# FFN 2 fused with router logits 1, linear attention fused with the reload and router logits 2, and a threshold search with two bits a round

## The chip, the cores and the metric

One core of a Trainium2 chip. The metric is device time in microseconds of one execution, the median of the runs. Engines: PE (TensorE), DVE (VectorE), ACT (ScalarE), POOL (GpSimd), SP (SyncE, which issues the plain DMAs).

## The reference

4096 tokens (4 batches of 1024) of 256 channels pass through six residual blocks in float32:

```
x = x + 0.5 * ffn(layernorm(x))
x = x + attention_over_sets(layernorm(x))
x = x + 0.5 * ffn(layernorm(x))          # FFN 2
x = x + 0.5 * moe(layernorm(x))          # routed experts, first time
x = x + linear_attention(layernorm(x))   # per batch: relu(q), relu(k), kv = k^T v
x = x + 0.5 * moe(layernorm(x))          # the same experts, second time
# inside moe, for the rows xf of layernorm(x), T = 4096, E = 32, cap = 160:
ri = concat(xf, mean, std, min, max, l2, share of |xf| < 1e-6)
h = gelu(ri @ r1_w.T + r1_b)
probs = softmax(h @ r2_w.T);  topp, topi = top_k(probs, 2)
score = where(routed, probs, -inf)
idx = argsort(-score, axis=0)[:cap].T    # each expert keeps its best 160 tokens
```

Each expert then runs a gated FFN on its 160 tokens, adds an adapter shared by two experts, and the weighted rows are added back to the tokens.

## The kernel before

The program is a row of stages (`Stage`), each with its own buffers and semaphores; a stage ends with a barrier of all engines. Inside a stage every engine runs its own list in order and waits on semaphores. x stays in SBUF as `x_res`, 32 tiles of 128 tokens; a group is 4 tiles, a batch 8. PSUM is 8 banks.

- `ffn` (L198 on): DVE normalizes a group (L194), PE transposes (L203), ACT copies (L294), PE multiplies (L270), POOL adds the bias (L226), DVE adds the product to x (L240) and takes the statistics (bn_stats, L163). Two groups are in flight.
- `moe` calls `route`, `experts` and, the first time, `reload`. `route` begins with the router front: variance over all 32 tiles on DVE (L171 to L183), one power on POOL for rstd (L188), two for the moments (L1341), then per group DVE norm, minimum, maximum (L1476, L1477) and the count under 1e-6 (L1480) from ACT's absolute value (L1367), PE's transposes, `hidden` (L1406, L1407), ACT's gelu (L1371), PE's logits (L1414) and DVE's copy of them (L1488). SP sends the expert weights first, then the rows of the normalized x, then x itself.
- The route proper begins at L1509: softmax, two picks a token, and the scores of 32 experts laid over 128 partitions (4 chunks an expert, 1024 columns). The search then finds each expert's 160th score bit by bit: 30 rounds, each a count by DVE, a sum over the four chunks by PE, and two small DVE operations:

```
nc.vector.tensor_scalar(above[:], score[:], thr[:].bitcast(F32), None, ALU.is_ge, ALU.add,
                        accum_out=count[:, 0:1]).then_inc(counted, 1)
v.wait_ge(totaled, k + 1)
```

- Behind the search come places, lists and indices for the gathers; `experts` runs 32 experts in quads, with weights loaded four experts ahead.
- `reload` (L1858) brings x back from `x_sum` in DRAM and takes its statistics. `linear_attention` takes one variance and one power over all tiles, then loops over the batches: norm, transposes (L2003), keys and values (L1974) with the running sum of k^T v (L1983), queries, the product with the output weights, the outputs (L1974), and DVE's update of x (L1945, L1946, L1948) with bn_stats (L1951). POOL adds the bias to the batch in one operation (L1918). PE runs ahead of DVE by the banks that it finds free.

Of the kernel before, what the change touches and what calls it, by code (L numbers as in the profile page):

```python
# [9 lines left out]

# [13 lines left out]
P = 128  # L24
# [4 lines left out]
GT = 4  # L29
# [1138 lines left out]
class RouterSetup:  # L1168
# [17 lines left out]
    def constants(self, nc, pool):  # L1186
# [22 lines left out]
        chain.link(nc.gpsimd.memset(s.half[:], 0.5))  # L1209

# [8 lines left out]
def alloc_moe(nc, s):  # L1219
# [12 lines left out]
    s.half = sb("half", [P, TILES], F32)  # L1232
    s.xn_rows = nc.dram_tensor("xn_rows", (TOKENS, ROW), F32, kind="Internal").ap()
# [3 lines left out]
def moe(nc, s, name, up_dram, down_dram, aup_dram, adown_dram, out=None):  # L1237


    st = Stage(nc, name)  # L1240
    w_up = [st.sb(f"w_up{k}", [P, CC, 2 * INTER]) for k in range(EQ)]
    w_down = [st.sb(f"w_down{k}", [P, INTER // P, C]) for k in range(EQ)]
    a_up = [st.sb(f"a_up{k}", [P, CC, 2 * A_INTER]) for k in range(EQ // 2)]
    a_down = [st.sb(f"a_down{k}", [P, C]) for k in range(EQ // 2)]
    of_pick = st.sb("of_pick", [P, QUADS_E, ST_TILES, 2])
    gather_i = st.sb("gather_i", [P, SLOT_TILES], I32)
    scatter_i = st.sb("scatter_i", [P, QUADS_E * 2 * ST_TILES], I32)
    w_in = [st.sem(f"w_in{k}") for k in range(EQ)]
    a_in = [st.sem(f"a_in{k}") for k in range(EQ // 2)]
    x_kept = st.sem("x_kept")  # L1250
    total = s.x_sum if out is None else out

    def load_expert(sp, e, k):

        sp.dma_start(w_up[k][:], up_dram[bass.ds(e, 1)].rearrange("o p c j -> (o p) c j")).then_inc(w_in[k], 16)
        sp.dma_start(w_down[k][:], down_dram[bass.ds(e, 1)].rearrange("o p c j -> (o p) c j")).then_inc(w_in[k], 16)

    def load_adapter(sp, g, k):
        sp.dma_start(a_up[k][:], aup_dram[bass.ds(g, 1)].rearrange("o p c j -> (o p) c j")).then_inc(a_in[k], 16)
        sp.dma_start(a_down[k][:], adown_dram[bass.ds(g, 1)].rearrange("o p j -> (o p) j")).then_inc(a_in[k], 16)  # L1260

    route(nc, s, name + "r", of_pick, gather_i, scatter_i, total, x_kept, load_expert, load_adapter)
    experts(nc, s, name + "e", w_up, w_down, a_up, a_down, w_in, a_in, of_pick, gather_i, scatter_i, total, x_kept,
            load_expert, load_adapter)
    if out is None:
        reload(nc, s, name + "c")
    st.close()
# [841 lines left out]
```

## Time and profile before

| | us |
|---|---|
| median of 3 timed runs | 2075.1 |
| lowest, highest | 2064.27, 2077.95 |
| the profiled execution | 2061.07 |
| its span | 2059.4 |
| busy in the span: PE | 1526.4 (74%) |
| DVE | 977.2 (47%) |
| ACT | 583.5 (28%) |
| POOL | 550.4 (27%) |

Mean granted TensorE clock 0.861 of full speed. Times of rows are from the start of the span. A row of a timeline gives start, busy time, engine, line, operation and tiles, and in brackets how long the engine had been idle and who ended that. "x8" means that eight like instructions in a row are merged in one line.

### The profile page before, as it was taken

The numbers are of one execution on the slowest core, as the hardware profiler recorded it, in microseconds if no ns is written. First come the engines' busy times: TensorE is split into PE (matmuls) and PEld (weight loads), VectorE is DVE, ScalarE is ACT, GpSimd is POOL, SyncE is SP. The second block draws the span as 40 slices with busy tenths as digits, with TensorE's granted clock in tenths as the row PEclk, the third lists the DMA queues.
The fourth block names the chain that finished last, engine by engine and source line by source line (L and its number), as shares of the span: only waits on it lengthen the run. The fifth ranks groups of instructions, "written<-read, shape, count | busy, mean of one in ns | idle before, by whom it ended". The sixth has DMA issues, their size and how long they took to land. (4 is left out here: it accounts for less than half of the span.)

```text
span 2059.4 us, 26489 instructions
## 1 busy us (share of the span) xinstructions
PE 1526.4 (74%) x9242; PEld 1139.1 (55%) x9242; DVE 977.2 (47%) x2391; ACT 583.5 (28%) x1295; POOL 550.4 (27%) x418
## 2 busy tenths in 40 slices
PE   2699889999996672238998894599763237999894
PEld 2567534545444541228898893356432226898894
DVE  5765677777754677671111110444367682111110
ACT  0122146665662141002323321111132002323321
POOL 2542200000003502002446336110111002346346
PEclk9899889999998886558999997799877557999997
DMA  2024463432100332004778774300133003778874
GB/s 90 16 87 136 103 111 59 77 72 50 45 2 1 121 105 81 0 0 141 221 215 231 228 189 52 104 0 0 63 136 102 5 0 101 241 209 212 254 208 51
DMA packets 114031, 212.12 MB, mean 103 GB/s; under 512 B 20149, under 2 KB 79962, under 8 KB 104730
## 3 DMA queue, kind: packets, MB, share of 16 engines
q1 hardware_dynamic: 87066, 178.93, 27.6%
q0 software_dynamic: 26880, 32.13, 10.4%
q8 instruction: 45, 0.74, 0.2%
q14 instruction: 40, 0.33, 0.1%
HBM read 158.71 MB, written 51.90 MB: 102 GB/s over the span
## 5 line engine op out<-in xcount | busy, mean ns | idle before, releaser
L907 DVE TENSOR_REDUCE attnm_top<-psum 128x1 f32<-128x384 f32 (+3 forms) x384 | 215.8, 596 | 70.6 <-PE psum L996 65.5
L1131 ACT ACTIVATE attnm_prob<-psum 128x512 f32<-128x512 f32 (+1 forms) x384 | 192.4, 530 | 132.5 <-PE psum L1006 127.3
L1843 DVE SCALAR_TENSOR_TENSOR moe1e_h<-moe1e_gate,psum 128x160 f32<-128x160 f32 x160 | 51.3, 321 | 261.6 <-ACT moe1e_gate L1801 261.6
L1718 POOL DMA_INDIRECT x_sum<-moe1e_y,moe_scatter_i x80 | 124.9, 1561 | 178.2 <-ACT moe1e_y L1825 112.4
L1843 DVE SCALAR_TENSOR_TENSOR moe2e_h<-moe2e_gate,psum 128x160 f32<-128x160 f32 x160 | 51.3, 321 | 252.5 <-ACT moe2e_gate L1801 252.5
L1718 POOL DMA_INDIRECT out<-moe2e_y,moe_scatter_i x80 | 125.1, 1564 | 170.0 <-ACT moe2e_y L1825 100.7
L1773 PE MATMUL psum<-moe1e_xgT,moe_w_up 128*128 128x160 f32 x1024 | 155.9, 314 | 10.4 <-issue 8.3
L1773 PEld LDWEIGHTS psum<-moe1e_xgT,moe_w_up 128*128 128x128 f32 x1024 | 151.0, 202 | 12.8 <-issue 12.8
L1773 PE MATMUL psum<-moe2e_xgT,moe_w_up 128*128 128x160 f32 x1024 | 150.4, 306 | 8.3 <-issue 6.1
L1773 PEld LDWEIGHTS psum<-moe2e_xgT,moe_w_up 128*128 128x128 f32 x1024 | 145.6, 196 | 10.1 <-issue 10.1
L994 PE MATMUL psum<-attn_mask_ts,ident_bf 128*128 128x128 bf16 x512 | 106.4, 228 | 15.5 <-DVE attnm_top L907 10.5
L893 POOL TENSOR_TENSOR attnm_tail_v<-attnm_v_tail,attnm_tail_p 128x256 f32<-128x256 f32 x32 | 19.8, 620 | 364.0 <-DVE attnm_on L954 299.3
L994 PEld LDWEIGHTS psum<-attn_mask_ts,ident_bf 128*128 128x128 bf16 x512 | 48.8, 99 | 114.9 <-issue 57.1
L996 PE MATMUL psum<-attnm_k_hat,attnm_q_hat 96*128 96x512 bf16 (+3 forms) x384 | 106.8, 306 | 0.0
L1006 PE MATMUL psum<-attnm_q_hat,attnm_k_hat 99*128 99x512 bf16 (+1 forms) x288 | 98.3, 344 | 0.0
L1019 PE MATMUL psum<-attnm_prob,attn_v_aug 128*32 128x512 f32 (+1 forms) x768 | 88.8, 533 | 0.0
L1801 ACT ACTIVATE moe1e_gate<-psum 128x160 f32<-128x160 f32 x160 | 48.5, 303 | 139.0 <-PE psum L1773 139.0
L1801 ACT ACTIVATE moe2e_gate<-psum 128x160 f32<-128x160 f32 x160 | 48.5, 303 | 131.1 <-PE psum L1773 131.1
L1785 PE MATMUL psum<-moe1e_h,moe_w_down 128*128 128x160 f32 x512 | 80.4, 300 | 2.6 <-ACT moe1e_yT L1808 2.6
L1785 PE MATMUL psum<-moe2e_h,moe_w_down 128*128 128x160 f32 x512 | 80.4, 300 | 2.6 <-ACT moe2e_yT L1808 2.6
L1785 PEld LDWEIGHTS psum<-moe2e_h,moe_w_down 128*128 128x128 f32 x512 | 72.9, 190 | 3.6 <-issue 3.6
L1785 PEld LDWEIGHTS psum<-moe1e_h,moe_w_down 128*128 128x128 f32 x512 | 72.9, 190 | 3.6 <-issue 3.6
(409 smaller groups left out, 2983.7 us busy)
## 6 DMA issues: line engine op xcount, KB each, us to landing
moe_w_up<-in_expert_up SPq DMA_DIRECT2D x64, 1024.0 KB, 5.6
moe_w_down<-in_expert_down SPq DMA_DIRECT2D x64, 512.0 KB, 7.0
attnm_q_hat<-q_parts SPq DMA_DIRECT2D x72, 128.0 KB, 4.8
moe_a_up<-in_adapter_up SPq DMA_DIRECT2D x32, 256.0 KB, 6.8
q_parts<-attnf_q_part SPq DMA_DIRECT2D x12, 512.0 KB, 2.8
attnm_k_hat<-k_parts SPq DMA_DIRECT2D x72, 64.0 KB, 2.3
x_res<-in_x SPq DMA_DIRECT2D x8, 512.0 KB, 8.5
v_tails<-attnf_v_tail SPq DMA_DIRECT2D x4, 1024.0 KB, 4.1
```

What stands on the lines that cost most here:

```text
L893: nc.gpsimd.tensor_tensor(tail_v[:, k % 2].rearrange("p (h d) -> p h d", d=HD), v_tail[:, b % 2, k].rearrange("p (h d) -> p h d", d=HD), t ...
L907: nc.vector.tensor_reduce(top[:, n // QUADS % 2, tiles[0]:tiles[-1] + 1, hh:hh + 1], s.ps[:, u.bank, 0:len(tiles) * width].rearrange("p (t ...
L994: nc.tensor.matmul(out[:, width - P:width], s.identb[:], o.mask_ts[:, tile % 2, :], start=(i == 0), stop=False, skip_group_check=True)
L996: ins = nc.tensor.matmul(out, q_hat[r][0:MROW, h, tile * P:(tile + 1) * P], k_hat[r][0:MROW, h, 0:width], start=False, stop=True, skip_gro ...
L1006: nc.tensor.matmul(s.ps[:, u.bank, at:GROUP], k_hat[r][0:MROW + NPART, h, j * P:(j + 1) * P], q_hat[r][0:MROW + NPART, h, g * GROUP + at:( ...
L1019: ins = nc.tensor.matmul(s.ps[32 * h:32 * h + 32, u.bank, at:GROUP], o.v_aug[:, first:first + 32], prob[:, i % NPROB, at:GROUP], start=(j ...
L1131: nc.scalar.activation(prob[:, i % NPROB, at:GROUP], s.ps[:, u.bank, at:GROUP], ACT.Exp).then_inc(taken[u.bank], 1)
L1718: nc.gpsimd.indirect_dma_start(total, bass.IndirectOffsetOnAxis(ap=scatter_i[:, at:at + 1], axis=0), y[:, q, k, :], None, bounds_check=TOK ...
L1773: ins = nc.tensor.matmul(s.ps[:, u.bank, half * CAP:(half + 1) * CAP], lhsT, xgT[:, q, c, k * CAP:(k + 1) * CAP], start=(c == 0), stop=(c ...
L1785: ins = nc.tensor.matmul(s.ps[:, u.bank, o * CAP:(o + 1) * CAP], lhsT, h[:, n % 2, i, :], start=(i == 0), stop=(i == PAIRS - 1))
L1801: nc.scalar.activation(gate[:, i, :], s.ps[:, u.bank, 0:CAP], ACT.Silu).then_inc(silu, 1)
L1843: nc.vector.scalar_tensor_tensor(out=h[:, n % 2, i, :], in0=gate[:, i, :], scalar=1.0 if i < INTER // P else SCALE_A, in1=s.ps[:, u.bank, ...
```

## The change

Lines move by one at the top and by more behind; the names of the tiles `moe1r_...` become `ffn_r_...` and `lin_r_...` where the router front moves.

1. The router front becomes a class, `RouterFront`, whose methods each issue one step for one group. Variance and powers are now taken per group (4 columns for rstd, 8 for the moments). The count under 1e-6 goes from DVE to ACT: Abs, Relu(1e-6 - |x|), and four Signs with an accumulator; ACT also copies the logits. SP stores x and the normalized rows group by group.
2. `ffn_router` replaces FFN 2 and the first router front. ACT now normalizes for FFN (Identity with scale and bias), and PE's order is a table.
3. `linear_router` replaces `reload`, `linear_attention` and the second front. Statistics, variance and rstd are taken per batch, the weights are loaded behind the first two groups of x, six PSUM banks rotate over all uses, and the front of batch b - 1 is laid between the steps of batch b.
4. The search takes two bits a round: the scores are split into their upper and lower 16 bits as floats, and a round tests three thresholds at once, one on DVE and two on ACT. POOL's products `value` come after its part of the conversion, so beside the search.

```diff
+    def count(self, act, g, ks):
+        act.wait_ge(self.near_made, g + 1)
...
+        for k in ks:
+            ins = self.nc.scalar.activation(self.size[:, g % 2, k, :], self.near[:, g % 2, k, :], ACT.Sign,
+                                            accum_out=self.stat[:, g % 2, k, 4:5])
...
+def ffn_router(nc, s, name, m):
...
+    for i in range(-2, GROUPS + 4):
+        for what, g in (("turn", i + 2), ("multiply", i + 1), ("turn_s", i - 2), ("hidden", i - 2), ("logits", i - 3), ("turn_x", i - 1)):
...
+            for i in range(GROUPS + 2):
+                if i < GROUPS:
+                    update(i)
+                    r.var(chain, i)
+                if i >= 2:
+                    r.finish(v, i - 2)
+                if 1 <= i <= GROUPS:
+                    r.moments(v, chain, i - 1)
+                    for k in range(GT):
+                        r.norm(v, i - 1, k)
+                    r.extremes(v, i - 1)
...
+            for i in range(-3, GROUPS + 4):
+                if 0 <= i + 3 < GROUPS:
+                    norm(i + 3)
+                if 0 <= i + 2 < GROUPS:
+                    copy(i + 2)
+                if 0 <= i - 2 < GROUPS:
+                    r.copy_s(act, i - 2)
+                    r.gelu(act, i - 2)
+                if 0 <= i - 3 < GROUPS:
+                    r.take(act, i - 3)
+                if 0 <= i - 1 < GROUPS:
+                    r.absolute(act, i - 1)
+                    r.under(act, i - 1)
+                    r.count(act, i - 1, range(GT))
+                    r.copy_x(act, i - 1)
...
-    ROUNDS = 30
...
+    HIGH = [4 ** k for k in range(6, -1, -1)]
+    LOW = [4 ** k for k in range(7, -1, -1)]
...
+                for i in (1, 3):
+                    ins = nc.scalar.activation(junk[i // 2], score[:], ACT.Sign, bias=tries[:, i:i + 1], scale=-1.0,
+                                               accum_out=under[:, i // 2 + 1:i // 2 + 2])
+                ins.then_inc(signed, 1)
...
+                pe.wait_ge(counted, k + 1)
+                pe.wait_ge(signed, k + 1)
+                nc.tensor.matmul(s.ps[:, 5, 0:3], s.same_e[:], under[:], start=False, stop=True).then_inc(totaled, 1)
...
+                    v.wait_ge(totaled, done + k + 1)
+                    chain.link(nc.vector.tensor_scalar(passed[:], s.ps[:, 5, 0:3], 0.0, None, ALU.is_le, ALU.add,
+                                                       accum_out=steps[:]))
...
+    def use():
+        return banks.use(next(ring) % 6)
...
+                for k in range(BT):
+                    ins = update(b, k)
+                    if k % GT == GT - 1:
+                        chain.link(ins)
+                        r.var(chain, BG * b + k // GT)
+                    if k == 2 and b >= 1:
+                        r.finish(v, r1)
+                if b + 2 < BATCH:
+                    stats(b + 2)
```

PE in FFN 2 and the router front, a middle stretch. Before, these are two stages, and in FFN 2 the row reads:

```order
L203 MATMUL psum<-ident,ffn_xn 128x128 x16
L270 MATMUL psum<-ffn_w,ffn_xnT 128x256 x8
L203 MATMUL psum<-ident,ffn_xn 128x128 x8
L270 MATMUL psum<-ffn_w,ffn_xnT 128x256 x8
L203 MATMUL psum<-ident,ffn_xn 128x128 x8
```

In the change one turn of the steady state reads so (the first two rows are FFN's for later groups, then the statistics, `hidden`, logits and transposes of earlier ones):

```order
L204 MATMUL psum<-ident,ffn_xn 128x128 x8
L1559 MATMUL psum<-ffn_w,ffn_xnT 128x256 x8
L1432 MATMUL psum<-ident,ffn_r_stat 5x128 x4
L1441 MATMUL psum<-ffn_r_xnT,r 128x512 x2
L1442 MATMUL psum<-ffn_r_statT,r1s 128x512
L1449 MATMUL psum<-r,ffn_r_hT 128x32 x4
L1423 MATMUL psum<-ident,ffn_r_xn 128x128 x8
```

The front's five PE steps now stand between FFN's multiply of one group and the transposes of the next.

PE in linear attention, the end of a batch, before (output of the batch is the last two rows, 8 tiles in all):

```order
L1974 MATMUL psum<-lin_w,lin_kvT 128x256 x4
L2033 REGISTER_ALU
L1974 MATMUL psum<-lin_kvw,lin_qT 128x257 x8
L1972 REGISTER_ALU
L1974 MATMUL psum<-lin_kvw,lin_qT 128x257 x4
```

and in the change, for batch 1 and later:

```order
L1423 MATMUL psum<-ident,lin_r_xn 128x128 x8
L2321 MATMUL psum<-lin_xnT,lin_w 128x512 x4
L2321 MATMUL psum<-lin_w,lin_kvT 128x256 x4
L2321 MATMUL psum<-lin_kvw,lin_qT 128x257 x6
L1432 MATMUL psum<-ident,lin_r_stat 5x128 x4
L1441 MATMUL psum<-lin_r_xnT,r 128x512 x2
L1442 MATMUL psum<-lin_r_statT,r1s 128x512
L2321 MATMUL psum<-lin_kvw,lin_qT 128x257 x6
```

The previous batch's router work stands between the queries and between the outputs (the second group's follows in the same way, then both logits).

DVE in the search, one round before:

```order
L1554 TENSOR_SCALAR moe1r_above,moe1r_count<-moe1r_score,moe1r_thr 128x1024
L1558 TENSOR_SCALAR moe1r_drop<-psum 128x1
L1559 SCALAR_TENSOR_TENSOR moe1r_thr<-moe1r_drop,moe1r_thr 128x1
L1554 TENSOR_SCALAR moe1r_above,moe1r_count<-moe1r_score,moe1r_thr 128x1024
L1558 TENSOR_SCALAR moe1r_drop<-psum 128x1
```

and the start and first round of the change:

```order
L1784 TENSOR_SCALAR moe1r_n_above<-moe1r_score 128x1024
L1785 TENSOR_SCALAR moe1r_n_equal<-moe1r_score 128x1024
L1807 COPY moe1r_level<-moe1r_tries 128x1
L1789 TENSOR_SCALAR moe1r_above,moe1r_under<-moe1r_score,moe1r_tries 128x1024
L1792 TENSOR_SCALAR moe1r_ahead<-tries_no,moe1r_tries 128x4
L1796 TENSOR_SCALAR moe1r_passed,moe1r_steps<-psum 128x3
L1798 SCALAR_TENSOR_TENSOR moe1r_tries<-moe1r_steps,moe1r_ahead 128x4
L1789 TENSOR_SCALAR moe1r_above,moe1r_under<-moe1r_score,moe1r_tries 128x1024
```

A round keeps one count on DVE; the two others are ACT's, between the same two waits.

## Rows read from the trace of the kernel before

**Rows 1.** Table of stretches; columns as its first line names them.
```profile
core 0: us, PE busy (x) PEld busy (x) DVE busy (x) ACT busy (x) POOL busy (x), PEclk, DMA share, GB/s
703.00:785.00 82.00, 48.16 (x208) 27.82 (x208) 47.15 (x152) 28.33 (x34) 16.82 (x4) 0.79 0.53 189
...
814.80:885.60 70.80, 17.58 (x60) 15.05 (x60) 48.17 (x121) 0.00 (x0) 1.55 (x1) 0.50 0.04 4
...
1303.00:1484.00 181.00, 161.01 (x560) 100.49 (x560) 73.21 (x219) 28.59 (x72) 23.59 (x6) 0.95 0.02 7
```

**Rows 2.** Timeline of FFN 2 (start us, us, engine, line, operation), one group.
```profile
675.17 2.37 POOL L226 TENSOR_TENSOR x_res<-x_res,ffn_bias 128x1024 f32 x1 [5.73 <-DVE ffn_xn L194]
...
675.25 1.22 DVE L240 TENSOR_TENSOR x_res<-x_res,psum 128x1024 f32 x1 [0.27 <-PE psum L270]
...
675.97 3.62 PE L270 MATMUL psum<-ffn_w,ffn_xnT 128*128 128x256 f32 x16
...
676.17 1.02 ACT L294 COPY ffn_xnT<-psum 128x1024 f32<-128x1024 f32 x1 [3.42 <-PE psum L203]
```

**Rows 3.** Timeline, router front 1, one group.
```profile
761.08 1.88 PE L1406 MATMUL psum<-moe1r_xnT,r 128*128 128x512 f32 x4
...
761.28 0.57 ACT L1361 COPY moe1r_statT<-psum 5x512 f32<-5x512 f32 x1 [0.23 <-PE psum L1397]
...
764.05 0.69 ACT L1371 ACTIVATE moe1r_hT<-psum,r1b 128x512 f32<-128x512 f32 x1 [2.20 <-PE psum L1407]
...
764.64 1.05 ACT L1367 ACTIVATE moe1r_work<-moe1r_xn 128x1024 f32<-128x1024 f32 x1
...
764.79 1.08 PE L1414 MATMUL psum<-r,moe1r_hT 128*128 128x32 f32 x8 [0.78 <-ACT moe1r_hT L1371]
```

**Rows 4.** Timeline, powers before both stages; the route's first reduction.
```profile
653.34 5.46 POOL L188 TENSOR_TENSOR rstd<-var_eps,minus_half 128x32 f32<-128x32 f32 x1 [9.68 <-DVE var_eps L183]
...
712.29 10.92 POOL L1341 TENSOR_TENSOR moe1r_moment<-moe1r_moment,half 128x32 f32<-128x32 f32 x2 [1.05 <-DVE moe1r_moment L1465]
...
784.50 1.22 DVE L1509 TENSOR_REDUCE moe1r_col<-moe1r_prob 128x32 f32<-128x1024 f32 x1
```

**Rows 5.** Timeline, second round of the first search.
```profile
817.27 1.28 DVE L1554 TENSOR_SCALAR_CACHE_REDUCE moe1r_above<-moe1r_score,moe1r_thr 128x1024 f32<-128x1024 f32 x1
...
818.62 0.59 PE L1433 MATMUL psum<-moe1r_count,same_e 128*128 128x1 f32 x2 [1.77 <-DVE moe1r_above L1554]
...
819.24 0.16 DVE L1558 TENSOR_SCALAR moe1r_drop<-psum 128x1 int32<-128x1 f32 x1 [0.68 <-PE psum L1433]
...
819.62 1.28 DVE L1554 TENSOR_SCALAR_CACHE_REDUCE moe1r_above<-moe1r_score,moe1r_thr 128x1024 f32<-128x1024 f32 x1
```

**Rows 6.** Timeline, from the reload to the second route.
```profile
1285.34 7.96 SPq L1858 DMA_DIRECT2D x_res<-x_sum  x8
...
1290.33 11.69 DVE L163 BATCH_NORM_STATS2 x_stats<-x_res 128x6 f32<-128x256 f32 x32 [39.29 <-DMA x_res<-x_sum]
...
1311.59 3.68 PE L2003 MATMUL psum<-ident,lin_xn 128*128 128x128 f32 x16 [52.21 <-DVE lin_xn L194]
...
1336.20 2.66 DVE L194 TENSOR_SCALAR lin_xn<-x_res,mean,rstd 128x256 f32 x8
...
1361.09 1.13 PE L1983 MATMUL psum<-lin_v_row,lin_k_row 128*128 128x257 f32 x4 [0.46 <-DVE lin_k_row L1929]
...
1377.69 2.66 DVE L194 TENSOR_SCALAR lin_xn<-x_res,mean,rstd 128x256 f32 x8
...
1482.15 0.43 DVE L1951 BATCH_NORM_STATS2 x_stats<-x_res 128x6 f32<-128x256 f32 x1
...
1566.01 1.22 DVE L1509 TENSOR_REDUCE moe2r_col<-moe2r_prob 128x32 f32<-128x1024 f32 x1
```

**Rows 7.** FFN 2's norm line (ns min/median/max); norms of router front 1.
```profile
L194 DVE TENSOR_SCALAR ffn_xn<-x_res,mean,rstd x12: 400/404/2464, 658.8 to 666.5; 128x256 f32<-128x256 f32 x8, 128x256 f32 x4
...
712.12 2.67 DVE L194 TENSOR_SCALAR moe1r_xn<-x_res,mean,rstd 128x256 f32<-128x256 f32 x8
```

More of the change, by code:

```diff
@@ L11 @@
+import itertools
 from contextlib import ExitStack
@@ L1565, in _ @@
+            search(LOW, len(HIGH))
+            chain.link(nc.vector.tensor_copy(level[:], tries[:, 1:2]))
+            nc.vector.tensor_scalar(above[:], score[:], level[:], None, ALU.is_gt, ALU.add, accum_out=count[:, 0:1])
+            nc.vector.tensor_scalar(equal[:], score[:], level[:], None, ALU.is_equal, ALU.add,
                                     accum_out=count[:, 1:2]).then_inc(tied, 1)
@@ new lines, in linear_router @@
+    u_T, u_kv, u_acc, u_q, u_turn, u_kvw, u_out, ring = {}, {}, {}, {}, {}, {}, {}, itertools.count()
+    def use():
+        return banks.use(next(ring) % 6)
+    for what, b, k in ORDER:
+        if what == "turn":
+            for c in range(CC):
+                u_T[b, k, c] = use()
+        elif what == "kv":
+            u_kv[b, k] = use()
+        elif what == "sum":
+            if k == 0:
+                for d in range(CC):
+                    u_acc[b, d] = banks.use(6 + d)
+        elif what == "q":
+            for f in range(CC):
+                u_q[b, k, f] = use()
+        elif what == "turn_kv":
+            u_turn[b] = use()
+        elif what == "kvw":
+            u_kvw[b] = use()
+        elif what == "out":
+            u_out[b, k] = use()
+        else:
+            r.plan(what, b, use)
@@ L1966, in _, with project @@
+            for g in range(BG * (BATCH - 1), GROUPS):
+                r.moments(v, chain, g)
+                for k in range(GT):
+                    r.norm(v, g, k)
+            for g in range(BG * (BATCH - 1), GROUPS):
+                r.extremes(v, g)
+                r.finish(v, g)
         @block.tensor
         def _(pe):
-            pe.wait_ge(w_in, 48)
-            pe.wait_ge(ones_made, 1)
-            def project(u, b, out, pairs):
-                pe.wait_ge(taken[u.bank], u.before(b))
+            def project(u, out, pairs):
+                pe.wait_ge(taken[u.bank], u.before(0))
@@ L2056, in linear_attention @@
+            r0, r1 = GROUPS - 2, GROUPS - 1
+            for g in (r0, r1):
+                r.absolute(act, g)
+                r.under(act, g)
+                r.count(act, g, range(GT))
+                r.copy_x(act, g)
+            for g in (r0, r1):
+                r.copy_s(act, g)
+                r.gelu(act, g)
+            for g in (r0, r1):
+                r.take(act, g)
     st.close()
```

899 lines of the change are left out of this document (600 added, 299 removed).

## The prediction

> **What bounds the kernel now.** The page's chain of waits reaches back only through the last expert stage, which the change leaves as it is, so I read by stretches first. The table of stretches [rows 1] shows three that the change touches: the front of the first router (PE busy 48 of 82 us, DVE 47 of 82: neither is full), the search (DVE busy 48 of 71, ScalarE 0, the granted clock at 0.50, which is the 1.2 GHz level, because PE has almost nothing to do), and linear attention (PE busy 161 of 181 at clock 0.95, close to 2.4 GHz: PE sets the pace). Then the timeline of each. FFN 2 is a ring of GpSimd's bias, PE's multiply, ScalarE's copy and DVE's update [rows 2]. The router front has no full engine; every group passes through DVE, PE and ScalarE in turn [rows 3], and before it begins everybody waits for long powers on GpSimd, one like FFN 2's of 5.46 us and then two in 10.92 us [rows 4]. A search round is a strict chain: count 1.28, a 128x1 matmul 0.59, two tiny DVE operations, and again 2.35 us later (819.62 - 817.27) [rows 5]. Thirty of them are the 70.8 us of rows 1, and the second router repeats them. In linear attention a batch takes 41.5 us (1377.69 - 1336.20), and before PE's first transpose at 1311.59 lie the reload from 1285.34 and 32 statistics in 11.69 us [rows 6].
>
> **Part 1: FFN 2 with router front 1.** Now it ends at 784.50, where the route proper starts [rows 4]. I count the fused stage by its fullest engine, group by group.
> ScalarE gets FFN's normalization (four 128x256 activations, the columns of Abs's 1.05 in four pieces, about 1.5), the copy 1.01, the statistics copy about 0.6, then it stands behind PE's `hidden` (761.08 to gelu's start at 764.05, 2.95) before gelu 0.69, takes the logits 0.3 (behind PE's 1.08), Abs 1.05, Relu 1.0, four accumulating Signs and two halves of the copy 1.1 [rows 2, 3]. No row shows an accumulating ScalarE operation. Below it is a plain one, a quarter of Abs's 1.05 or 0.3 with its start; above, three times that; I take 0.45, 1.8 for four. Sum: 12.4 us a group; 10.9 without the normalization, 9.9 without the first copy (the last groups).
> PE: transposes 1.0, multiply 3.6, transposes again 1.0, statistics 0.5 with 0.7 of waiting for their copy, hidden 2.95, logits 1.0 = 10.7. DVE: update 1.2, four bn_stats 1.4, variance and moments 13 tiny ones of 0.16 to 0.2, 2.4 in all, norm 1.4, minimum and maximum 2.4 (two reductions of 1024 columns at 1.22 [rows 4]), rest 0.4 = 9.2. GpSimd: 2.4 of bias and, at 5.46/32 = 0.17 us a column, 2.1 of powers = 4.5. So ScalarE sets the pace.
> Fill: rstd is ready at about 659 (653.34 and 5.46 [rows 4]), the first hidden ends near 693 (update 0 at 670, norm 0 at 681, counts 685, finish 688, then 4 us on PE). From there 2 x 12.4 + 10.9 + 4 x 9.9 = 75 to the last hidden at 768, 2.5 for the last gelu, logits and copy, 1.1 for the change of stage: 772 against 784.5. **-13 us**, between -26 (DVE's 9.2 as the pace) and +3 (dear Signs).
>
> **Part 2: the reload, linear attention and router front 2.** Now from 1285.34 to 1566.01 [rows 6].
> Start: PE waits for 8 tiles of statistics instead of 32 (24 x 0.365 = 8.8 saved) and for a power over 8 columns instead of 32 (about 4 saved); the change of stage between goes too (1.2), and the weights, now queued behind two groups of x, come about as late as the first transposed tile (0 to 5 lost). -12.6.
> Batch 0: DVE gets two variances (2 x 1.5) and the statistics of batch 2 (8 x 0.365 and 1.4) behind its updates. There is no slack there: PE already waits 0.46 for DVE's next key at 1361.09. +7.3.
> Batches 1 to 3: PE gets per batch two each of transposes 0.95, statistics with their copy 1.1, hidden 2.7 and logits 0.95 = 11.4. It was the pace, so all of it is path. +13 for batch 1 (statistics of batch 3 behind it), +11.4 for batch 2, +8 for batch 3, whose last updates, DVE-bound before, now have only two tiles left to do once PE is through. What hides beside PE: DVE's norm, extremes and finish (some 11 us a batch) and ScalarE's Abs, Relu, Signs (4 us), spread over 55 us. If that cover goes, see the second rival.
> End: from the last update (1482.6) to 1566.01 there are 83.4 us now, the whole front 2. After, only the last two groups: variance, power, moments and norm 4.6 for the first, then ScalarE's 5 for each, the two hidden with gelu 8, logits and copies 2.5, some 26, and 1.2 for the stage. -56.
> Sum: -12.6 + 7.3 + 13 + 11.4 + 8 - 56 = -29. I add 3 for queueing between in-order engines (0 to 20). **-26 us.**
> SP's stores are moved too: 1 MB a group, behind var and norm, on a queue that stands idle then; the expert weights are issued only at the start of the route, a good 100 us before their use. Both cost nothing, and the search is their cover.
>
> **Part 3: the search, twice.** The order shows 7 + 8 = 15 rounds with one DVE count and two ScalarE counts each. No row shows a 128x1024 Sign with accumulation. Below stands Abs at 1.05 [rows 3], two of them overlapped 2.0; above, 1.7 each. I take 2.25 for the pair, near the row. DVE's own 1.28 count hides behind it. The rest of the round stays: from the count's end to the next count 1.06 (matmul 0.59 and the tiny ones), 0.1 for one more accumulator read, 0.06 to start ScalarE. 3.47 x 15 = 52 against 70.7. Added: two integer operations on 1024 columns (0.6 to 1.3 each), one 1.05 conversion and 0.4 small, 3.0; in the middle two DVE passes and a restart, 2.7; the level copy 0.2. 57.9: **-12.8 us** each, between -19 and +8 (4.7 a round). GpSimd's bf16 products now run beside the first rounds instead of beside DVE's last steps ahead of them: I count that as nothing (-2 to +4). Two searches, -25.6.
>
> **Sum.** -13 - 26 - 25.6 = -65. The profiled execution took 2061.1 (its span is 2059.4), the three timed runs 2064.3 to 2078.0 with the median 2075.1, 14 above it. So 1996 for an execution like the profiled one, **2010** for the median.
>
> **The shared port.** One norm of 128x256 in FFN 2 took 2464 ns where its median is 404, just where GpSimd's 2.35 us bias add ran; eight norms under the long power took their usual 2.67 [rows 7]. So a bias add stops DVE's norms and a power does not. The Trainium skill (SBUF — State Buffer, Who interferes with whom) says that a DVE operation in a two-port mode and a GpSimd operation exclude each other for a whole instruction, which speaks against giving GpSimd and DVE more to do side by side. The bias add agrees with it, the power does not. In the fused FFN the bias add falls, by the order, mostly on minimum and maximum; in linear attention on updates that read PSUM. By the trace I add nothing; by the rule it would be the last rival.
>
> **Rivals.**
> 1. ScalarE's accumulator is dear, 0.5 us more for each. FFN: 2 us a group, +16; search: 1.0 a round, 15 x 2, +30; the end of linear attention +4. That leaves 15: 2060. For: nothing shows its price. Against: DVE's own accumulator read is tiny, its 1.28 count being hardly longer than the plain reduction of 1024 columns, 1.22 [rows 4, 5].
> 2. The in-order queues of linear attention hold each other up: PE stands behind turn_s and its copy, ScalarE behind hidden, DVE behind the counts, and each batch is 6 us longer. 47 left: 2028. For: PE already runs 89% busy. Against: six rotating banks.
> 3. Slower: GpSimd blocks DVE with everything it does in the fused stages. FFN 8 x 4.5 = 36; linear attention 4 bias adds of twice 2.37 and 22 of powers, 41; in each search four products and a conversion of 1024 columns, at the bias row's 2.4 each, 12, twice 24: 101 in all, +36: 2111. It turns the sign once more than 65 of the 101 lie on the path. For: the 2464 ns norm. Against: norms under the power.
>
> **How the numbers follow.** Forecast 0.68, rival 1 0.08, rival 2 0.21, rival 3 0.03. A measurement tells about 1% (21 us) from no change. Faster by over 1%: forecast, rival 2 and a fifth of rival 1, 0.91; within 1% 0.06; slower 0.03. The range: with every part at its best, 26, 29 and 2 x 19, they save 93 (1982); upward the range goes past rival 2 to 2042.
>
> **What would show it.** Route 1's first reduce 12 to 14 us earlier after the end of attention (131 us after FFN 2's rstd begins at 653.34 become some 119); search rounds of 3.4 to 3.6 us with ScalarE the last releaser of PE; 255 us from the reload to route 2, batches of 53 to 55. Wrong if a round takes over 4.2, if ScalarE is not the fullest engine of the fused FFN, or if a batch takes 60.

## The result, and the profile after

The changed kernel takes 1999.7 us (median of four runs, 1990.8 to 2004.3), against 2075.9 before in the same runs: the ratio is 0.968, with a 95% interval from 0.963 to 0.972 (the two medians alone would give its lower edge). A second measurement (e5_again below) gave 0.968 again (0.963 to 0.974). The forecast was 2010 of 2075.1, a ratio of 0.969. The profiled execution took 2000.8 (span 1999.1), where 1996 was forecast for an execution like the profiled one of before. ScalarE's busy time rose from 583.5 to 719.5 us:

```profile
PE 1537.6 (77%) x9242; PEld 1145.6 (57%) x9242; DVE 917.0 (46%) x2376; ACT 719.5 (36%) x1625; POOL 564.7 (28%) x454
```

The sum came out; its parts did not all. Between marks that both traces have (times in us):

| Stretch | before | after | difference | forecast |
|---|---|---|---|---|
| start to FFN 2's rstd power | 653.3 | 647.3 | -6.1 | 0 |
| stage 1: from there to route 1's first reduction | 131.2 | 134.7 | +3.6 | -13 |
| route 1, to the count after the search | 101.0 | 86.4 | -14.6 | -12.8 |
| from there to the reload (experts) | 399.8 | 396.2 | -3.6 | 0 |
| reload to route 2 | 280.7 | 247.5 | -33.1 | -26 |
| route 2, to the count after the search | 101.0 | 86.4 | -14.6 | -12.8 |
| from there to the end | 392.4 | 400.5 | +8.1 | 0 |

The three stretches that the change does not touch moved by -6.1, -3.6 and +8.1 and nearly cancel. The first and the last go with the granted clock (from 100 to 300 us it is 0.92 instead of 0.90, in the last 200 us 0.88 instead of 0.93). So a stretch is worth a few us more or less from one execution to the next, and parts are read from their own marks.

**Stage 1.** The table of stretches of the changed kernel, columns as in [rows 1], cut where the last FFN multiply ends (738), and at the end of linear attention:

```profile
core 0: us, PE busy (x) PEld busy (x) DVE busy (x) ACT busy (x) POOL busy (x), PEclk, DMA share, GB/s
647.30:702.00 54.70, 38.14 (x165) 27.61 (x165) 30.81 (x104) 32.35 (x62) 32.08 (x16) 0.81 0.20 68
702.00:738.00 36.00, 32.96 (x158) 24.10 (x158) 22.20 (x68) 23.76 (x54) 9.69 (x6) 0.92 0.26 88
738.00:782.00 44.00, 31.25 (x80) 16.13 (x78) 10.74 (x38) 18.72 (x47) 4.58 (x4) 0.51 0.11 36
...
1485.30:1512.20 26.90, 14.99 (x52) 7.82 (x52) 10.04 (x35) 12.47 (x31) 4.34 (x3) 0.71 0.18 59
```

Two things stand against the prediction. ScalarE is nowhere the fullest engine. And from 738 the granted clock is 0.51, the 1.2 GHz level, in a stretch where nobody is full. The timeline shows group 5 there (start us, us, engine, line, operation, idle time before it and its releaser):

```profile
736.29 0.69 ACT L1408 ACTIVATE ffn_r_hT<-psum,r1b 128x512 f32<-128x512 f32 x1 [3.30 <-PE psum L1442]
...
741.47 0.17 DVE L1365 TENSOR_SCALAR ffn_r_stat<-ffn_r_stat 128x4 f32<-128x4 f32 x1 [1.70 <-ACT ffn_r_size L1383]
...
741.70 1.02 PE L1432 MATMUL psum<-ident,ffn_r_stat 128*5 128x128 f32 x4 [3.53 <-DVE ffn_r_stat L1365]
...
742.75 0.57 ACT L1401 COPY ffn_r_statT<-psum 5x512 f32<-5x512 f32 x1 [0.36 <-PE psum L1432]
743.58 3.75 PE L1441 MATMUL psum<-ffn_r_xnT,r 128*128 128x512 f32 x4 [0.86 <-ACT ffn_r_statT L1401]
747.26 2.07 PE L1442 MATMUL psum<-ffn_r_statT,r1s 5*128 5x512 f32 x2
749.37 0.69 ACT L1408 ACTIVATE ffn_r_hT<-psum,r1b 128x512 f32<-128x512 f32 x1 [6.04 <-PE psum L1442]
```

Read it as a ring, that is, a loop in which each engine waits for what the next one makes from its own last result: ScalarE counts, VectorE finishes, TensorE transposes the statistics, ScalarE copies them, TensorE multiplies (hidden: here 5.8 us, in rows 3 still 3.0), and only the gelu lets ScalarE go on to the next group's Abs, Relu and counts. While ScalarE counts, TensorE waits 3.53; while TensorE multiplies, ScalarE waits 6.04.

**Search.** One steady round of the changed kernel's first search; compare [rows 5]:

```profile
840.15 1.15 ACT L1694 ACTIVATE moe1r_work<-moe1r_score,moe1r_tries 128x1024 f32<-128x1024 f32 x1 [3.39 <-DVE moe1r_tries L1812]
840.15 1.28 DVE L1789 TENSOR_SCALAR_CACHE_REDUCE moe1r_above<-moe1r_score,moe1r_tries 128x1024 f32<-128x1024 f32 x1
...
841.30 1.13 ACT L1694 ACTIVATE moe1r_work<-moe1r_score,moe1r_tries 128x1024 f32<-128x1024 f32 x1
...
842.67 0.56 PE L1711 MATMUL psum<-moe1r_under,same_e 128*128 128x3 f32 x2 [1.91 <-ACT moe1r_work L1694]
843.26 0.16 DVE L1796 TENSOR_SCALAR_CACHE_REDUCE moe1r_passed<-psum 128x3 f32<-128x3 f32 x1 [1.68 <-PE psum L1711]
...
843.66 1.28 DVE L1789 TENSOR_SCALAR_CACHE_REDUCE moe1r_above<-moe1r_score,moe1r_tries 128x1024 f32<-128x1024 f32 x1
```

A round is 843.66 - 840.15 = 3.51 us for two bits, where one bit took 2.35, and what releases TensorE is ScalarE's second count.

**Linear attention.** From the reload to route 2, the rows that answer to [rows 6]:

```profile
1264.68 0.93 SPq L2188 DMA_DIRECT2D x_res<-x_sum  x2
...
1276.14 3.65 PE L2330 MATMUL psum<-ident,lin_xn 128*128 128x128 f32 x16 [38.81 <-DVE lin_xn L195]
...
1318.43 1.81 PE L2330 MATMUL psum<-ident,lin_xn 128*128 128x128 f32 x12
...
1328.88 1.89 PE L2349 MATMUL psum<-lin_v_row,lin_k_row 128*128 128x257 f32 x4 [3.13 <-DVE lin_k_row L2246]
...
1377.68 1.94 PE L2330 MATMUL psum<-ident,lin_xn 128*128 128x128 f32 x16
...
1432.28 1.94 PE L2330 MATMUL psum<-ident,lin_xn 128*128 128x128 f32 x16
...
1485.31 0.43 DVE L2272 BATCH_NORM_STATS2 x_stats<-x_res 128x6 f32<-128x256 f32 x1
...
1512.21 1.22 DVE L1740 TENSOR_REDUCE moe2r_col<-moe_prob 128x32 f32<-128x1024 f32 x1 [14.41 <-PEq L57]
```

From transpose to transpose the batches take 42.3, 59.3 and 54.6 us (41.5 for a batch before), the last one 53.0 to its last update, and from there route 2 is 26.9 us away (83.9 before).

### The profile page after: what moved, and what is told of

Same layout as the page of the kernel before. It is cut to its first block and busy times, and to the rows that moved or that the text cites. A ratio compares the mean times of both kernels' runs of the same rounds, so it can differ in the third digit from the quotient of the medians.

```text
span 1999.1 us, 26485 instructions
## 1 busy us (share of the span) xinstructions
PE 1537.6 (77%) x9242; PEld 1145.6 (57%) x9242; DVE 917.0 (46%) x2376; ACT 719.5 (36%) x1625; POOL 564.7 (28%) x454
## 5 line engine op out<-in xcount | busy, mean ns | idle before, releaser
L2028 PE MATMUL psum<-moe2e_xgT,moe_w_up 128*128 128x160 f32 x1024 | 158.2, 317 | 8.5 <-issue 6.3
L2028 PEld LDWEIGHTS psum<-moe2e_xgT,moe_w_up 128*128 128x128 f32 x1024 | 153.4, 204 | 10.5 <-issue 10.5
L995 PE MATMUL psum<-attn_mask_ts,ident_bf 128*128 128x128 bf16 x512 | 106.3, 228 | 15.5 <-DVE attnm_top L908 11.1
L997 PE MATMUL psum<-attnm_k_hat,attnm_q_hat 96*128 96x512 bf16 (+3 forms) x384 | 106.7, 306 | 0.0
```

Source lines behind the costliest of these rows:

```text
L995: nc.tensor.matmul(out[:, width - P:width], s.identb[:], o.mask_ts[:, tile % 2, :], start=(i == 0), stop=False, skip_group_check=True)
L997: ins = nc.tensor.matmul(out, q_hat[r][0:MROW, h, tile * P:(tile + 1) * P], k_hat[r][0:MROW, h, 0:width], start=False, stop=True, skip_gro ...
L2028: ins = nc.tensor.matmul(s.ps[:, u.bank, half * CAP:(half + 1) * CAP], lhsT, xgT[:, q, c, k * CAP:(k + 1) * CAP], start=(c == 0), stop=(c ...
```

## The experiments

"Stage 1" is the time from FFN 2's rstd power to route 1's first reduction. A ratio is against runs of the kernel before that were made beside the experiment; "filler" is a matmul whose result nobody reads.

**e1_split.** Only FFN 2 and router front 1 are taken apart.

```diff
-    ffn_router(nc, s, "ffn2", m)
+    ffn(nc, s, "ffn2")
+    front(nc, s, "front", m)
```

`ffn` and the front are the code of the kernel before.

> The changed kernel with FFN 2 and the first router's front taken apart again (the stages and the code of the kernel before), linear attention and the search as changed. Stage 1 is the time from the start of FFN 2's rstd power to the first reduction of route 1: 131.2 us before, 134.7 after. Theory A (the fusion hides FFN 2's work but gives it back, because every group is one serial loop of ScalarE and TensorE in which TensorE waits and its clock falls to 1.2 GHz): stage 1 comes back to 131 to 133, so the whole kernel is 0 to 5 us faster than the changed one, about 1995 to 2000. Theory B (the fusion did save the 13 us of the prediction, and something upstream of it or a disturbed run hid that): stage 1 is 144 to 148 and the whole is 10 to 15 us slower, about 2012.

Measured: stage 1 146.8 us, but the whole 2007.4, ratio 0.971 (0.965 to 0.977). The stage's number is theory B's, the reason isn't: here the unfused front itself ran at a low clock. The profiled execution is also the slowest of the four (1989.3 to 2013.9), so its stage need not be the one of the others. Its FFN 2 took as long as before, its front 94.0 us from the power to the route instead of 78.7:

```profile
core 0: us, PE busy (x) PEld busy (x) DVE busy (x) ACT busy (x) POOL busy (x), PEclk, DMA share, GB/s
...
745.00:797.00 52.00, 45.79 (x152) 25.89 (x151) 24.46 (x80) 16.13 (x21) 0.00 (x0) 0.70 0.37 121
```

**e2_filler.** Matmuls that nothing reads, where TensorE waits in the last three groups.

```diff
             for what, g in ORDER:
+                if what == "turn_s" and g >= GROUPS - 3:
+                    pe.wait_ge(taken[u_t[GROUPS - 1].bank], u_t[GROUPS - 1].after(0))
+                    for _ in range(3):
+                        nc.tensor.matmul(s.ps[:, 0, :], s.ident[:], ffn_w, start=True, stop=True)
```

> The changed kernel, with three matmuls of 128x512 into a free bank ahead of TensorE's transposes of the statistics for the last three groups of FFN 2's fused stage; nothing reads them. They fill the 2.7 to 3.5 us in which TensorE waits there. Theory A (the clock is the cause): it stays at 2.4 GHz and the periods from gelu to gelu of the last three groups fall from 13.1, 13.9 and 13.9 us to 9.9 to 10.3 each; stage 1 goes from 134.7 to 121 to 124, the whole is 11 to 13 us faster. Theory C (the periods are ScalarE's own work or a wait on GpSimd or VectorE, and the clock only follows): the periods stay at 13 to 14 us, or grow by the filler, and the whole is the same or up to 5 us slower.

Measured: stage 1 121.9 us, 12.8 less; the whole 1981.4, ratio 0.963 (0.956 to 0.970). The stretch of the last groups of e2_filler, then its last four gelus:

```profile
core 0: us, PE busy (x) PEld busy (x) DVE busy (x) ACT busy (x) POOL busy (x), PEclk, DMA share, GB/s
...
743.00:774.20 31.20, 24.46 (x98) 12.10 (x96) 10.75 (x38) 18.56 (x47) 4.58 (x4) 1.00 0.15 51
```

```profile
741.30 0.69 ACT L1408 ACTIVATE ffn_r_hT<-psum,r1b 128x512 f32<-128x512 f32 x1 [3.30 <-PE psum L1442]
751.22 0.69 ACT L1408 ACTIVATE ffn_r_hT<-psum,r1b 128x512 f32<-128x512 f32 x1 [3.30 <-PE psum L1442]
761.13 0.69 ACT L1408 ACTIVATE ffn_r_hT<-psum,r1b 128x512 f32<-128x512 f32 x1 [3.30 <-PE psum L1442]
771.05 0.69 ACT L1408 ACTIVATE ffn_r_hT<-psum,r1b 128x512 f32<-128x512 f32 x1 [3.30 <-PE psum L1442]
```

More work on TensorE, and the stage is shorter: the clock stays at 1.00, the periods (from one gelu to the next) are 9.92 us. Theory A holds, C falls.

**e3_order.** Another order on ScalarE in the same stage (the `if`s on each group stay).

```diff
+                    r.copy_s(act, i - 2)
                     norm(i + 3)
                     copy(i + 2)
-                    r.copy_s(act, i - 2)
+                    r.absolute(act, i - 1)
+                    r.under(act, i - 1)
                     r.gelu(act, i - 2)
                     r.take(act, i - 3)
-                    r.absolute(act, i - 1)
-                    r.under(act, i - 1)
                     r.count(act, i - 1, range(GT))
                     r.copy_x(act, i - 1)
```

> The changed kernel with another order on ScalarE in FFN 2's fused stage: the statistics copy first, then FFN's normalization and copy and the next group's Abs and Relu, and only then the gelu, so that this work (up to 5.3 us) lies beside TensorE's hidden product of 3.0 us. Theory A (a serial loop: ScalarE idles 3.3 us behind hidden, TensorE idles 3.5 us behind the counts): at 2.4 GHz a group with FFN's multiply takes 11 to 11.5 us, one without 7.7 to 8.5; stage 1 is 108 to 114, the whole 20 to 26 us faster; if the clock still falls in the last groups, they take 10 to 11 and the whole is 13 to 17 faster. Theory C (ScalarE's amount of work is the pace, as the prediction summed it, whatever the order): its work is unchanged, and the whole moves by less than 5 us.

Measured: stage 1 116.8 us, 17.9 less; the whole 1978.2, ratio 0.961 (0.957 to 0.965). ScalarE's work is the same, so its amount was not the pace: the ring was. The groups with an FFN multiply take 8.7 to 10.6 us, the last three 10.8, 10.5 and 9.6, since the clock still fell there (0.61 on average). Against the changed kernel the first four periods are 10.6 us shorter and the last three 10.0, and the first gelu comes 2.7 later:

```profile
core 0: us, PE busy (x) PEld busy (x) DVE busy (x) ACT busy (x) POOL busy (x), PEclk, DMA share, GB/s
702.00:738.00 36.00, 32.73 (x164) 22.18 (x162) 30.12 (x94) 28.46 (x66) 14.60 (x10) 1.00 0.34 117
738.00:771.00 33.00, 27.02 (x78) 13.96 (x78) 9.11 (x27) 15.58 (x38) 3.54 (x2) 0.61 0.14 48
```

**e4_onebit.** Both fusions, the search of before (`for k in range(ROUNDS)` with ROUNDS = 30 on VectorE and TensorE, no counts on ScalarE).

> The changed kernel with the search of the kernel before (one bit a round, 30 rounds, no halves), both fusions kept. Theory (the two-bit search is worth what the traces show in each route): from the route's first reduction to the count after the search 99 to 101 us instead of 86.4, the whole 26 to 30 us slower, about 2027. Rival (GpSimd's products, which now run beside the search instead of beside the steps ahead of it, give part of the gain, and that part stays with either search): the route takes 97 or 98 us, the whole is 20 to 24 us slower.

Measured: each route 100.9 us, the whole 2033.5, ratio 0.986 (0.982 to 0.990), so 1.8% of some 2065 or 37 us above the changed kernel's, more than the 26 to 30 expected; its stage 1 (136.3) and its reload to route 2 (250.4) were 2 and 3 us longer as well. The routes, 2 x 14.5 us, give the theory's number. The rival isn't tested by it: with this search GpSimd's products again start beside the steps ahead of it.

**e5_again.** The changed kernel once more.

> The changed kernel once more, as it is, beside the others of this call, for a second profile of it. In FFN 2's fused stage the clock has fallen to 1.2 GHz in the last three groups in both profiles that have this stage unchanged. If that belongs to the schedule, it does so again: stage 1 (start of FFN 2's rstd power to route 1's first reduction) 133 to 137 us, the last three periods between gelus 13 to 14 us. If it is chance, stage 1 is 121 to 125 us this time. Whole against before 0.965 to 0.971.

Measured: stage 1 134.7 us, last periods 13.1, 13.9 and 13.9; reload to route 2 251.7; ratio 0.968. The low clock belongs to the schedule: all five profiles that have this stage unchanged (after, e4, e5, e6, e12) show 134.7 to 136.4. In three of them (e4, e6, e12) the seven periods are 13.7, 15.5, 14.0, 9.9, 11.9, 13.1 and 13.9, so the clock also falls earlier on, and the total is nearly the same.

**e6_linear.** Two moves in linear attention. The diff shows the first (after each fourth key the variance of that batch follows); the second is on ScalarE behind the last batch, where copy_s of group 6 comes ahead of group 7's Abs and Relu, and those ahead of group 6's gelu.

```diff
                 for k in range(BT):
                     keys(b, k)
+                    if b == 0:
+                        far, pair = 2 + k // 4, 2 * (k % 4)
+                        v.wait_ge(x_in[BG * far + pair // GT], 16)
+                        for tile in (BT * far + pair, BT * far + pair + 1):
+                            ins = nc.vector.bn_stats(s.stats[:, tile, :], s.x[:, tile, :])
...
-                if b + 2 < BATCH:
-                    stats(b + 2)
```

> The changed kernel with two moves in linear attention. First: the statistics of the tiles of batches 2 and 3 are taken between the keys of batch 0, where VectorE waits 2.2 us each time, instead of behind the last updates of batches 0 and 1. Second: after the last batch ScalarE copies the statistics of group 6 before it starts on group 7's Abs and Relu. Theory (the stall of TensorE behind VectorE's key at the start of batch 1, 3.1 us, and the 5.1 us ahead of hidden for group 6 are queues in order, no work): batch 1 (59.3 us from transpose to transpose) takes 54 to 56, the time from the last update to route 2 falls from 26.9 to 22 to 24, and reload to route 2 from 247.5 to 239 to 242. Rival (batch 1 is long by TensorE's own work and by its clock): batch 1 stays at 58 or more, and only the end moves.

Measured: reload to route 2 243.5 us (239 to 242 expected) against 251.7 of e5_again beside it, whole 1984.8, ratio 0.961 (0.956 to 0.965). Batch 1 now takes 54.2, batch 2 52.4:

```profile
1316.25 1.80 PE L2339 MATMUL psum<-ident,lin_xn 128*128 128x128 f32 x12
...
1370.41 1.95 PE L2339 MATMUL psum<-ident,lin_xn 128*128 128x128 f32 x16
```

The first move holds. The second gave 1.6 us only (from the last update to route 2 30.6 instead of 32.2, not 22 to 24).

**e7_all.** e3's order, e6's moves and one filler matmul of 128x512 in the last three groups.

> The changed kernel with ScalarE's new order in FFN 2's fused stage, the two moves in linear attention, and one matmul of 128x512 into a free bank ahead of the statistics' transposes of the last three groups (1.0 us in waits of 1.25 us). Theory: the parts add up. Stage 1 108 to 111 us if the clock now stays at 2.4 GHz (periods of 7.7 to 8.2 in the last three groups), 115 to 117 if one short matmul doesn't hold it; reload to route 2 239 to 242 us; whole 28 to 34 us faster than the changed kernel, about 1965 to 1970. Rival (what is won in one stage is given back in the next, since the routes and experts take their own time from their own waits): the whole gains less than 20.

Measured: 1962.1 us, ratio 0.949 (0.944 to 0.954), 34.7 below e5_again beside it. Stage 1 106.7, with 7.6 us for each of the last groups; reload to route 2 243.5. 28.0 + 8.3 = 36.3: the parts add up, and at most 1.6 is given back, which is less than the spread of the runs. The end of linear attention is what stayed slow:

```profile
core 0: us, PE busy (x) PEld busy (x) DVE busy (x) ACT busy (x) POOL busy (x), PEclk, DMA share, GB/s
...
1449.40:1478.90 29.50, 20.46 (x52) 10.11 (x52) 8.99 (x29) 12.61 (x31) 4.33 (x3) 0.55 0.16 54
...
730.00:756.00 26.00, 21.13 (x101) 11.63 (x100) 10.49 (x38) 17.70 (x46) 4.54 (x3) 1.00 0.18 61
```

**e8_split_filler.** e1_split with a matmul of 128x256 into the free bank ahead of each wait for the gelu.

> The kernel of e1_split (FFN 2 and the first router's front in stages of their own) with one matmul of 128x256 into a free bank (0.5 us at 2.4 GHz) where TensorE waits 0.78 us for the gelu. In e1_split the front ran at a clock that went up and down (0.54 and 0.70) and took 94.0 us from its rstd power to route 1, the same code of before took 78.7 at a clock of up to 0.97. Theory (the same front has two paces, by the clock alone, and it hangs on how much TensorE does in its waits): with the filler the clock stays up, periods are 6.8 to 7.0 us, and stage 1 is 131 to 134 us instead of 146.9. Rival (e1_split's front was slow by something else, such as its buffers or its DMAs): stage 1 stays at 144 or more.

Measured: stage 1 135.6 us (131 to 134 expected, 144 by the rival), periods 8.7 once and then 6.8; whole 2000.3, ratio 0.970 (0.963 to 0.977). The clock came back:

```profile
731.00:782.00 51.00, 45.52 (x195) 25.55 (x194) 29.99 (x97) 20.59 (x26) 0.00 (x0) 0.93 0.41 134
```

That the filler did it isn't shown, since e10_linear_only has the same front without filler and ran at the fast pace too (132.1), and this profile is of the fastest of four executions (1988.6 to 2010.8).

**e9_end.** e7_all with four fillers of 128x512 at each of two places behind the last batch.

> The kernel of e7_all with four matmuls of 128x512 into a free bank at two places behind linear attention's last batch: ahead of group 6's transposes, where TensorE waits 4.0 us for VectorE's norm, and ahead of group 7's transposes of the statistics, where it waits 2.6 us at 1.2 GHz. In e7_all the granted clock of the last 30 us ahead of route 2 is 0.61 and 0.50, and hidden takes 5.8 us instead of 3.0. Theory (the clock falls because TensorE waits, and fillers hold it there too): the clock stays near 1.0, hidden takes 3.0, the time from the last update to route 2 falls from some 30 us to 21 to 24, reload to route 2 from 243.5 to 235 to 238, whole 6 to 9 us faster than e7_all, about 1955. Rival (behind the last batch too little work is left on TensorE for any filler of this size to hold the clock): hidden stays at 5.8 us, and the fillers at 1.2 GHz delay what comes behind them by up to 8 us.

Measured: 1965.3 us, ratio 0.950 (0.946 to 0.955); reload to route 2 242.6, the same as e7_all within a microsecond. The rival: hidden of group 6 still takes 5.8 us, the second filler 6.6, and only then is the clock high again for group 7 (3.0).

```profile
1459.05 3.75 PE L1441 MATMUL psum<-lin_r_xnT,r 128*128 128x512 f32 x4 [0.87 <-ACT lin_r_statT L1401]
1462.73 2.07 PE L1442 MATMUL psum<-lin_r_statT,r1s 5*128 5x512 f32 x2
1464.73 6.64 PE L2415 MATMUL psum<-lin_w,ident 128*128 128x512 f32 x8
...
1472.68 1.95 PE L1441 MATMUL psum<-lin_r_xnT,r 128*128 128x512 f32 x4 [0.87 <-ACT lin_r_statT L1401]
```

**e10_linear_only.** e1_split's and e4_onebit's edits together: only linear attention's fusion is left.

> The changed kernel with both other parts taken out: FFN 2 and router front 1 in stages of their own, and the search of before with one bit a round; linear attention with the reload and router front 2 stays fused. Theory (linear attention's fusion gives 33 us by itself, as the two traces show from the reload to route 2): reload to route 2 247 to 252 us, routes 101 us each; where front 1 keeps its clock (stage 1 131 to 136) the whole is 29 to 33 us faster than before, about 2031; where it loses it (147) 15 to 20 faster. Rival (part of these 33 us is the first route's or the search's doing, for example because the fused stage before leaves the experts' data elsewhere): reload to route 2 takes 260 or more.

Measured: reload to route 2 250.1, stage 1 132.1, routes 101.0; whole 2032.3, ratio 0.984 (0.979 to 0.989), which is 33 us of 2066. The theory's numbers.

**e11_search.** e9_end with two matmuls of 128x256 in each search round.

> The kernel of e9_end with two matmuls of 128x256 into a free bank in each round of the search, between the product that waits for nothing and the one that waits for the counts (TensorE idles 1.9 us there, the clock is 0.50). Theory (TensorE's small product and its way to VectorE, 0.56 us and 0.6 in all at 1.2 GHz, lie on the round's path and get shorter at 2.4 GHz): the clock rises to 1.0 in the search, a round takes 3.2 to 3.3 us instead of 3.51, the whole is 5 to 9 us faster than e9_end. Rival (the clock stays at 0.50 in the search, since two short matmuls a round are too little): a round takes 3.5 to 3.7 and the whole is the same or up to 6 us slower.

Measured: the route takes 86.4 us as before, whole 1967.2, ratio 0.952 (0.947 to 0.957). The clock did not rise:

```profile
790.00:846.00 56.00, 45.71 (x120) 31.40 (x120) 29.81 (x93) 35.47 (x60) 10.88 (x5) 0.50 0.00 1
```

**e12_products.** GpSimd's products wait for the end of the search (`pool.wait_ge(tied, 1)`).

> The changed kernel with GpSimd's four products (and nothing else) held back until the search is over. In the changed kernel they run beside the first rounds, where two tiny VectorE operations take 0.55 and 1.36 us instead of 0.23 and 0.16. Theory (GpSimd's products block VectorE's operations that only touch SBUF wherever they run): from the first count to the count after the search 54.9 to 55.2 us instead of 56.5, and behind it the products lengthen VectorE's passes over 1024 columns: from there to the first gather's transposes 51 to 55 us instead of 49.6. Rival (the long tiny operations are something else): the search keeps its 56.5 us, and the stretch behind it its 49.6.

Measured, in a single execution: route 1 up to the count after the search 85.2 us instead of 86.4 (55.3 of it from the first count, 54.9 to 55.2 expected), from there to the gather's transposes 52.8 instead of 49.6. The scans that took 2.35 and 2.33 now take

```profile
876.03 2.85 DVE L1825 TENSOR_TENSOR_SCAN moe1r_n_above<-moe1r_one,moe1r_base,moe1r_above 128x1024 f32<-128x1024 f32 x1
876.72 4.82 POOL L1679 TENSOR_SCALAR moe1r_value<-moe1r_pick,row_no 128x1024 bf16<-128x1024 f32 x1
878.80 3.13 DVE L1826 TENSOR_TENSOR_SCAN moe1r_n_equal<-moe1r_one,moe1r_base,moe1r_equal 128x1024 f32<-128x1024 f32 x1
```

The theory holds: it is the products, wherever they run. The whole took 2022.0 us, some 22 more than the changed kernel. Of that, 13 lie between the search and the reload, of which 3.2 are those above; for the rest the granted clock of the experts is lower (0.95 instead of 1.00 over one stretch of 100 us). With one execution it isn't shown whether that belongs to the edit.

## Why the prediction was right, and where it was wrong

**The whole** came out (0.969 forecast, 0.968 twice), and that it came so close is luck: part 1 lost what parts 2 and 3 won beyond the forecast, +16.6 against -7.1 and -3.5, and the stretches that the change leaves alone gave -1.6. The two profiled executions are 60.3 us apart where 65 was forecast, the medians 76. The prediction added to its forecast the 14 us by which the profiled execution of before lies under its median; after the change the two agree within 1.1 us.

**Part 1 was wrong**, and the step that failed is "ScalarE sets the pace", with its falsifier in the text. ScalarE's sum held at 2.4 GHz: 10.9 and 9.9 us a group were forecast, 10.8 and 9.9 came (gelu to gelu from 715.6 to 736.3). In part that is luck: the items as listed add up to 12.0 and not to the 12.4 written, and the wait for hidden measured 3.30 where 2.95 stood. And these 3 us were not ScalarE's work, they were "then it stands behind PE's hidden", taken as constant from [rows 3]. What I had summed was a ring through three engines. In a ring each engine waits for the others, so TensorE has gaps of 3.5 us, and in them the clock fell; hidden then took 5.8. The account from the first gelu to the last is 89.4 us against 75 forecast: +11.2 from the three groups at 1.2 GHz (13.1, 13.9, 13.9), +3 from the first two periods (14.2 and 13.6 instead of 12.4; FFN's four activations took 2.08, not 1.5, and the clock dipped once, from about 698 to 708). The rest of the 16.6 lies ahead (0.9 in the fill) and behind (1.2). e2 shows the cause, since filling the gaps gives the 12.8 back; e3 shows the ring, since reordering the same work gives 17.9; 10.6 of that came in the first four periods and 10.0 in the last three, less 2.7 in the fill, and how much of the 10.0 is order and how much clock is not separated.

The fusion itself is worth nothing measurable in this form: unfused, stage 1 takes 131.2, 146.8, 135.6 and 132.1 us (before, e1, e8, e10), fused 134.7 to 136.4; the ratios are 0.971 and 0.970 unfused, 0.968 and 0.968 fused. With the clock held in the last groups the fused form is 9.2 shorter (131.2 against e2's 121.9), where 13 was forecast.

**Part 2** was right in its mechanism, short by 7.1. Start -14.8 (forecast -12.6: TensorE's first transpose 11.5 us behind the reload instead of 26.3, and the weights were not late). Batches +38.6 (forecast 42.7 with queueing; 170.6 from first transpose to last update became 209.2). Of the +7.3 that I gave batch 0 less than 1 shows there (42.3 against 41.5). Batch 1 grew by 17.8 instead of 13, and in it TensorE waits 3.13 for a key behind the statistics of batch 2; with e6 it takes 54.2. Batch 1 was near the 60 of my falsifier, the two after it at 54.6 and 53.0 as said. End -57.0 (forecast -56). In other executions the end takes 30 to 32 us instead of 26.9, at a lower clock (0.60 in e5, 0.68 in e10, 0.71 here), and the fusion is then worth 29 to 31; so some 3 us of the 7.1 are this execution's.

**Part 3** was right. Forecast for a round 3.47, measured 3.51, with ScalarE as the last releaser. ScalarE's pair of counts took 2.4 with its last accumulator read (2.25 forecast), the middle 2.3 (2.7). At the upper end, 4.7 a round, the prediction's own terms make a search 5.7 us longer, not 8. The term that was off is the products, "counted as nothing (-2 to +4)". [rows 5] begin too late to show it: before, while the products ran, two of VectorE's steps ahead of the search were long. In the timeline of the kernel before they are

```profile
806.10 2.81 DVE L1533 TENSOR_TENSOR moe1r_prob<-moe1r_prob,moe1r_key 128x1024 f32<-128x1024 f32 x1
807.82 3.82 POOL L1350 TENSOR_SCALAR moe1r_xn<-moe1r_pick,row_no 128x1024 bf16<-128x1024 f32 x1
808.94 2.23 DVE L1536 SCALAR_TENSOR_TENSOR moe1r_above<-moe1r_key,moe1r_prob 128x256 f32<-128x256 f32 x4
...
811.70 1.87 DVE L1542 TENSOR_SCALAR moe1r_col<-moe1r_col 128x32 f32<-128x32 f32 x1
```

and in that of the changed kernel

```profile
803.59 1.23 DVE L1764 TENSOR_TENSOR moe_prob<-moe_prob,moe1r_key 128x1024 f32<-128x1024 f32 x1
804.85 1.43 DVE L1767 SCALAR_TENSOR_TENSOR moe1r_above<-moe1r_key,moe_prob 128x256 f32<-128x256 f32 x4
```

These two steps give -2.4. Two small operations behind them (1.87 and 1.08 us, 0.18 and 0.22 after) held the first count 0.6 us behind the copy of the scores, 0.1 after, so -0.5. With the conversions (+2.5) the stretch up to the first count is 29.95 us instead of 30.35. In the first two rounds the products cost +1.2, as e12 shows by taking them away (55.3 instead of 56.5); the search takes 56.5 instead of 70.7. So the products' move gave -1.7 in each route, inside its own bounds and about what part 3 won beyond its forecast.

**The rivals.** Rival 1 (dear accumulators) fell: a counting Sign of 128x256 starts 0.40 us after the one ahead of it, one of 128x1024 1.15, and most of the read beside it (0.19) overlaps. Rival 2 (queues in linear attention, 6 us a batch) fell as a sum, +38.6 being under the forecast, but its mechanism is real in batch 1. Rival 3 fell in the fused stages: no update, norm or reduction there was longer than alone (the eight reductions of stage 1 at L1357 take 1.220 to 1.223). One step of a variance was: it took 2.05 us instead of 0.17 beside the first bias add of linear attention (1277.33 to 1281.85),

```profile
1279.83 2.05 DVE L172 TENSOR_TENSOR mean<-x_stats 128x8 f32<-128x8 f32 x1
```

but TensorE's first product of keys and values still came 7.8 us behind its first transpose (8.1 before), so it cost nothing. What the price hangs on is the kind of VectorE operation beside GpSimd: products and bias adds beside operations with two inputs in SBUF cost (above, and e12's scans, 2.33 to 3.13), bias adds beside reductions do not. The Trainium skill (SBUF — State Buffer, Who interferes with whom) says just that: an operation with two SBUF inputs contends with GpSimd's reads, a reduction never does. I had cited only the rule on two-port modes from that section; the other one would have found the 2.4 us ahead of the search, and the rows here agree with it. It isn't only operations with two inputs that waited: the small one at L1542 reads one tile and took 1.87 us beside a product of 1.91, as the norm of 2464 ns had done beside a bias add.

**What stays open.** Why the unfused front kept 2.4 GHz in three profiles and lost it in e1. Whether a larger filler, or one placed earlier, would hold the clock behind linear attention's last batch; e9 only shows that these two don't. Whether the 10 us that e12 lost among the experts are its own.

## What to carry to other kernels

Before you add up the work of one engine, follow one group through all of them: where an engine's order makes it wait for a result that another engine makes from its own last one, the period is the ring, and moving work that is ready into that wait (e3: 17.9 us for an edit of order alone) is worth more than the fusion (9.2 us with the clock held). A stage that gets fuller in its sum can get emptier on TensorE, so give a predicted stage a price at both clock levels. And read what runs beside GpSimd's elementwise work before you move it: it costs where it goes.

The best version is e7_all, 5.1% below before and 2.0% below the changed kernel.

## What the runs showed of the hardware

- Work that nobody reads can shorten a stage: three 128x512 matmuls a group kept the granted clock at 1.00 where it had been 0.51 (e2). In e11 TensorE was busy 45.7 of 56 us and the clock stayed at 0.50, in e2 24.5 of 31.2 at 1.00; in e2 the clock was high when the stretch began, in the search it was low.
- The same front (in one of them with a filler) ran 6.8 us a group in three executions and some 8.5 in a fourth, where hidden's products of 2.5 and 3.4 us alternated, and 1.9 is what they take at the high clock (e1).
- Of ScalarE's activations of 128x256 with a scale and a bias per partition one starts 0.49 us after the other (four in 2.08), of its counting Signs 0.40.
- A GpSimd operation can hold a small VectorE operation for almost its whole length: 128x32 took 1.87 us instead of 0.18, 128x8 2.05 instead of 0.17.
